# Seven of a head's complement masks by adding DMAs, their tiles taken later; output stores by sync

## Chip, cores and metric

One core of one Trainium2 chip. The metric is the device time of an execution in microseconds (us); the time before is the median of three runs.

## The reference, cut to what matters

Two graph layers over 2048 nodes with 512 features, each after a layer norm and a relu, each added to x. The first layer (related pairs, softmax over 1500 nodes, aggregation) is not touched. The second is an attention of 16 heads with a dense adjacency mask:

```
seq = (x @ W_seq).reshape(N, H, DH)              # N 2048, H 16, DH 32
scores = leaky_relu(score1[:, :, None] + score2[:, None, :], 0.2)
scores = scores + (1.0 - adj)[None, :, :] * MASK_VAL
attn = softmax(scores, axis=-1)
hidden = einsum('hij,jhd->ihd', attn, seq).reshape(N, D_IN) @ W_out + b_out
x = x + elu(hidden)
```

With leaky relu the exponential of a score is one of two products of a factor of i and a factor of j, by the sign of the sum. So a head needs, for each tile j of 128 columns, a mask of the neighbours whose sum is positive, and the rest of the neighbours: its complement within the adjacency.

## The kernel before

**Stages.** Stages 1 and 2 (to about 634 us) do the first layer, the projection to seq and the scores; `Heads` makes the factors, stores the score rows to DRAM and loads them back spread over the partitions. `stage4` (L1370 to 1616) is the 16 heads, `Output` (L1619 on) the last projection, elu and the stores.

**A head of stage 4.** Each head has 16 tiles j. `masks[:, j]` is one byte (fp8) per i, 2048 columns. ScalarE makes the sign mask of 13 tiles (L1443), VectorE that of tiles 3, 8 and 13 (`vector_sign`, L1484); VectorE ands each with the transposed adjacency `adjT` (`mask`, L1493), in the order 0 to 15. TensorE takes tile j in one of two ways. A **far** tile (the ten of `FAR`) has its own complement mask in `fars`: for each block of 128 rows it runs two matmuls of 99 columns, L1595 with the mask and L1596 with the complement. A **near** tile has none: L1598 multiplies the mask with 198 columns and L1599 the constant negated adjacency `nadjT` with 99. Complements come from `complement` (L1394): VectorE makes eight by xor (`far`, called one tile late), GpSimd two (tiles 3 and 5, `POOL_FAR`) by subtraction.

**Order.** TensorE walks j = 0 to 15 in two halves of the rows; the second half runs `LAG` = 4 tiles behind the first, so a head is 32 half-steps. A half fills four banks of psum; VectorE reduces them (`sum_parts`, L1506) in the middle of the next head, after its masks 3 and 5, and gives them free (`bank_free`), which the next head's first matmul of that half waits for. A mask slot may be written again when the second half has used it (`mask_used`; for the last tile `psum_done[1]`). VectorE also makes the values of the next head (`values`, two `take_off`), packed by ScalarE (`pack`, L1432), and scales, joins and norms the head before.

**Queues.** SP loads the row of scores of head n + 2 when head n's masks are all made (1 MB after spreading), and the x tiles for the output. GpSimd makes its complements and later issues the sixteen output stores (L1727). In stage 2 SP's last stores of x come before `heads.sync`, which stores the score rows (L1276) and loads the first two (L1280).

Of the kernel before, what the change touches and what calls it, by code (L numbers as in the profile page):

```python
# [20 lines left out]
U8 = mybir.dt.uint8  # L21
F8 = mybir.dt.float8e4
# [449 lines left out]
def stage2(nc, c, io, t, s, ps, f, heads, begin):  # L472
# [55 lines left out]
    with nc.Block() as block:  # L528
        @block.sync
        def _(sp):  # L530
# [77 lines left out]
            heads.sync(sp)  # L608
# [476 lines left out]
        def _(dve):  # L1085
# [135 lines left out]
            dve.wait_ge(masked, HA * ET)  # L1221
            for i, j in enumerate(NEAR_TILES):
# [142 lines left out]
NS = NT - len(VECTOR_SIGN)  # L1365
# [4 lines left out]
def stage4(nc, c, io, t, s, ps, output):  # L1370
# [18 lines left out]
    pool_far = sem("pool_far")  # L1389
    summed, scaled, joined, inverse = sem("summed"), sem("scaled"), sem("joined"), sem("inverse")  # L1390
    normed = t["normed"]

# [5 lines left out]
    with nc.Block() as block:  # L1398
        @block.sync
        def _(sp):  # L1400
# [5 lines left out]
            for n in range(HB - 2):  # L1406
                sp.wait_ge(mask_ready, NT * (n + 1))
                load(n + 2, n % 2)
# [5 lines left out]
            for b in (2, 3):  # L1414
                output.load(sp, b)

        @block.gpsimd
        def _(pool):
            for n in range(HB):
                for j in POOL_FAR:  # L1420
                    pool.wait_ge(mask_ready, NT * n + j + 1)
                    complement(pool, j, ALU.subtract).then_inc(pool_far, 1)
            output.gpsimd(pool)

        @block.scalar
        def _(act):
# [7 lines left out]
            def head(n, b):  # L1434
                act.wait_ge(s1_in[b], 8 * (n - b) + 16)
                for j in range(NT):
                    if j not in VECTOR_SIGN:

                        if j < NT - 1:
                            act.wait_ge(mask_used, (NT - 1) * n + j + 1)  # L1440
# [6 lines left out]
                    if j in (9, 14) and n < HB - 1:  # L1447
                        pack(n + 1, 1 - b, 0 if j == 9 else 1)
# [5 lines left out]
        def _(dve):  # L1454
# [26 lines left out]
            def vector_sign(n, b, j):  # L1481
                dve.wait_ge(mask_used, (NT - 1) * n + j + 1)
# [4 lines left out]
            def mask(n, j):  # L1487
                if j in VECTOR_SIGN:
                    dve.wait_ge(vector_signs, len(VECTOR_SIGN) * n + VECTOR_SIGN.index(j) + 1)
                else:  # L1490
                    dve.wait_ge(signs, NS * n + sum(x not in VECTOR_SIGN for x in range(j)) + 1)
# [42 lines left out]
            def head(n, b):  # L1534
                for j in range(NT):
                    if j + 1 in VECTOR_SIGN:
# [4 lines left out]
                    if n > 0:  # L1541
                        if j == 3:
                            sum_parts(n - 1, 0)
                        if j == 5:
# [8 lines left out]
                    if n < HB - 1:  # L1553
                        if j == 1:
                            values(n + 1)
                        if j == 9:
                            take_off(n + 1, 1 - b, 0)
                        if j == 11:
# [17 lines left out]
        def _(pe):  # L1576
            pe.sem_inc(mask_used, NT - 1)  # L1577

            def step(n, b, half, j):

                base = 4 * half
                if j == 0:
                    pe.wait_ge(bank_free[half], n + 1)
                pe.wait_ge(mask_ready, NT * n + j + 1)
                if j in POOL_FAR:
                    pe.wait_ge(pool_far, len(POOL_FAR) * n + POOL_FAR.index(j) + 1)
                elif j in FAR:
                    pe.wait_ge(far_ready, len(VECTOR_FAR) * n + VECTOR_FAR.index(j) + 1)
                for i in range(HT):
                    cols = slice(half * HALF + i * P, half * HALF + (i + 1) * P)  # L1590
                    out = ps[:, base + i // 2, 256 * (i % 2):256 * (i % 2) + 3 * CZ].rearrange("p (s c) -> p s c", s=3)
                    first = dict(start=(j == 0 and i % 2 == 0), stop=False, skip_group_check=True)
                    then = dict(start=False, stop=(j == NT - 1), skip_group_check=True)
# [6 lines left out]
                if j == NT - 1:  # L1600
                    last.then_inc(psum_done[half], 1)
                if half and j < NT - 1:
# [16 lines left out]
class Output:  # L1619
# [104 lines left out]
    def gpsimd(self, pool):  # L1724
        for it in range(NT):
            pool.wait_ge(self.done, it + 1)
            pool.dma_start(self.out[it * P:(it + 1) * P, :], self.x(it)).then_inc(self.y_out, 16)  # L1727
        pool.wait_ge(self.y_out, 16 * NT)


def build(nc, io, out, kind="Internal"):
# [4 lines left out]
        "adj_chunks": dram("adj_chunks", [NT, P, N], F8),  # L1736
    }
    with ExitStack() as c:
# [7 lines left out]
        t["adjT_in"], t["seq_in"] = (c.enter_context(nc.semaphore(n)) for n in ("adjT_in", "seq_in"))  # L1746
        t["rstd"] = c.enter_context(nc.sbuf_tensor("rstd", [P, 2, NT], F32))
# [50 lines left out]
```

## Time and profile before

| | us |
|---|---|
| median of three runs | 1166.32 (1164.46 to 1168.64) |
| the profiled execution | 1169.42 |
| its span | 1167.0 |
| busy: TensorE, VectorE, ScalarE, GpSimd | 1080.7, 949.3, 809.0, 163.1 |
| stage 4, about | 634 to 1096 |

The mean granted clock of TensorE is 0.979 of full speed. Busy time of TensorE is modelled from its matmuls' starts, and a few per cent of its records can be missing, so pace is read from starts. "By starts" below means from one instruction's start to the next one's on the same engine.

### The profile page before, as it was taken

How to read it: one execution, taken by the hardware profiler on the slowest of the kernel's cores; microseconds unless marked ns; L12 is line 12 of the kernel's file. 1: busy time of each engine (PE TensorE's matmuls, PEld its weight loads, DVE VectorE, ACT ScalarE, POOL GpSimd, SP SyncE). 2: the span in 40 equal slices, each digit the busy share in tenths (PEclk: the TensorE clock that was granted, in tenths of full speed). 3: DMA queues.
4: the chain of work that ended last, by engine and by line, in shares of the span. 5: the costliest groups of instructions: out<-in, count | busy, mean ns of one | idle time of the engine just before them, and what ended most of it. 6: DMA issues, size and time to landing. Idle time of an engine off the chain costs nothing. (4 is left out here: it accounts for less than half of the span.)

```text
span 1167.0 us, 24746 instructions
## 1 busy us (share of the span) xinstructions
PE 1080.7 (93%) x10565; PEld 738.8 (63%) x10565; DVE 949.3 (81%) x1323; ACT 809.0 (69%) x843; POOL 163.1 (14%) x174
## 2 busy tenths in 40 slices
PE   1999986999999999999996999999999999999997
PEld 1444432444444444444443999999999999999743
DVE  2355336899999999998834899999999999999565
ACT  1334326677777777775525999999999999999122
POOL 2788640000000000000000100100110000000011
PEclk9999996999999999999997899999999999999999
DMA  9630452322221121000433011110111111111311
GB/s 340 142 26 2 110 104 68 75 57 66 66 66 43 42 57 57 28 37 27 163 126 131 38 38 38 38 39 38 38 38 38 39 38 38 38 39 38 110 72 72
DMA packets 38269, 77.69 MB, mean 67 GB/s; under 512 B 5653, under 2 KB 15250, under 8 KB 36114
## 3 DMA queue, kind: packets, MB, share of 16 engines
q1 hardware_dynamic: 31954, 67.62, 16.1%
q0 software_dynamic: 6208, 8.50, 6.0%
q8 instruction: 84, 1.38, 0.5%
q14 instruction: 23, 0.19, 0.1%
HBM read 65.39 MB, written 23.21 MB: 76 GB/s over the span
## 5 line engine op out<-in xcount | busy, mean ns | idle before, releaser
L1443 ACT ACTIVATE area_h<-area_a,keep 128x2048 fp8e4<-128x2048 f32 x208 | 396.9, 1987 | 0.5 <-PEq L1577 0.5
L1595 PE MATMUL psum<-s_V,area_h 128*128 128x99 bf16 x2560 | 254.5, 210 | 21.1 <-issue 10.9
L1595 PEld LDWEIGHTS psum<-s_V,area_h 128*128 128x128 fp8e4 x2560 | 237.4, 98 | 25.2 <-issue 22.8
L1598 PE MATMUL psum<-s_V,area_h 128*128 128x198 bf16 x1536 | 218.7, 249 | 0.0
L1599 PE MATMUL psum<-s_V,late 128*128 128x99 bf16 x1536 | 212.8, 209 | 0.0
L1596 PE MATMUL psum<-s_V,area_b 128*128 128x99 bf16 x2048 | 205.5, 210 | 0.0
L1596 PEld LDWEIGHTS psum<-s_V,area_b 128*128 128x128 fp8e4 x2048 | 190.3, 98 | 0.0
L737 PE MATMUL psum<-area_h,f_region 128*128 128x512 f32 x384 | 184.9, 596 | 0.0
L1493 DVE TENSOR_TENSOR area_h<-area_h,area_a 128x512 uint32<-128x512 uint32 x256 | 173.5, 688 | 9.1 <-ACT area_h L1443 4.6
L1159 DVE SCALAR_TENSOR_TENSOR f_region<-area_b,s_r,f_region 128x1500 f32<-128x1500 f32 x96 | 170.8, 1780 | 2.2
L1170 DVE CUSTOM_DVE_ANT_0 area_b<-psum,late 128x1500 f32<-128x1500 f32 x96 | 161.1, 1715 | 10.8 <-PE psum L652 10.6
L956 ACT ACTIVATE area_b<-area_b,s_negm 128x1500 f32<-128x1500 f32 x96 | 147.8, 1541 | 25.4 <-DVE s_negm L1170 24.3
L652 PE MATMUL psum<-area_a 64*128 64x512 f32 (+1 forms) x576 | 143.5, 633 | 14.0 <-DVE s_negm L1170 13.9
L1598 PEld LDWEIGHTS psum<-s_V,area_h 128*128 128x128 fp8e4 x1536 | 150.4, 98 | 0.2
L1599 PEld LDWEIGHTS psum<-s_V,late 128*128 128x128 fp8e4 x1536 | 150.1, 98 | 0.0
L156 POOL DMA_INDIRECT rel_planes<-f_ones,f_flat x80 | 99.8, 1247 | 56.0 <-issue 20.4
L1394 POOL TENSOR_TENSOR area_b<-area_a,area_h 128x512 uint32<-128x512 uint32 x32 | 41.0, 1281 | 452.8 <-DVE area_h L1493 452.8
L652 PEld LDWEIGHTS psum<-area_a 64*128 64x128 f32 x576 | 55.0, 198 | 76.0 <-issue 52.2
L737 PEld LDWEIGHTS psum<-area_h,f_region 128*128 128x128 f32 x384 | 65.0, 191 | 43.0 <-issue 43.0
L902 ACT ACTIVATE f_region<-psum 128x256 f32<-128x256 f32 x96 | 36.6, 381 | 79.5 <-PE psum L707 63.9
L431 PE MATMUL psum<-f_region 128*128 128x512 f32 x192 | 83.7, 595 | 5.3 <-DVE f_region L304 4.1
L431 PEld LDWEIGHTS psum<-f_region 128*128 128x128 f32 x192 | 36.1, 190 | 49.8 <-issue 43.3
(175 smaller groups left out, 1343.5 us busy)
## 6 DMA issues: line engine op xcount, KB each, us to landing
area_a<-s_rows SPq DMA_DIRECT2D x16, 1024.0 KB, 4.6
rel_planes<-f_h SPq DMA_DIRECT2D x3, 2304.0 KB, 15.9
late<-rel_planes SPq DMA_DIRECT2D x36, 192.0 KB, 2.6
area_h<-in_x SPq DMA_DIRECT2D x4, 1024.0 KB, 12.9
keep<-in_adj POOLq DMA_DIRECT2D x16, 256.0 KB, 6.6
f_region<-in_x SPq DMA_DIRECT2D x16, 256.0 KB, 4.7
x<-f_region SPq DMA_DIRECT2D x16, 256.0 KB, 2.0
area_a<-adj_chunks SPq DMA_DIRECT2D x4, 1024.0 KB, 9.1
```

The lines of the kernel that those rows point to most:

```text
L431: last = pe.matmul(ps[:, 4 + g % 4, :], wT[w][:, k, dt * P:(dt + 1) * P], hT[:, k, ch * 512:(ch + 1) * 512], start=(k == 0), stop=(k == KT ...
L652: return pe.matmul(ps[:, 3 * half + ch, 0:cols.stop - cols.start], qk[rows, Q, p, r * P:(r + 1) * P], qk[rows, K, p, cols], start=True, st ...
L737: last = pe.matmul(ps[:, 7 if r < ET - 1 else 0, :], WT[m % 2][:, b, :], h[:, 2 * m + b, :], start=(m == order[0] and b == 0), stop=(m == ...
L956: act.activation(ex[:, hd, 0:NREL], ex[:, hd, 0:NREL], ACT.Exp, bias=negm[:, b, hd:hd + 1], scale=-1.0, accum_out=zs[:, b, hd:hd + 1]).the ...
L1159: dve.scalar_tensor_tensor(w, ex[:, hd, 0:NREL], r8[:, hd:hd + 1], w, ALU.mult, ALU.add).then_inc(added if hd < HA - 1 else w_ready, 1)
L1170: dve.tensor_tensor_reduce(ex[:, hd, 0:NREL], ps[:, 3 * (hd % 2):3 * (hd % 2) + 3, :].rearrange("p c j -> p (c j)")[:, 0:NREL], low[r % 2] ...
L1443: act.activation(masks[:, j, :], s1b[:, b, :], ACT.Relu, bias=t["s2"][:, n, 0, j:j + 1], scale=BIG, saturate=False).then_inc(signs, 1)
L1493: dve.tensor_tensor(own, own, adjT[:, :, j, :].bitcast(U32), ALU.bitwise_and).then_inc(mask_ready, 1)
L1595: pe.matmul(out[:, :, 0:DZ], masks[:, j, cols], V[:, b, j, :, 0:DZ], **first)
L1596: last = pe.matmul(out[:, :, DZ:CZ], fars[FAR.index(j)][:, cols], V[:, b, j, :, DZ:CZ], **then)
L1598: pe.matmul(out, masks[:, j, cols], V[:, b, j, :, :], **first)
L1599: last = pe.matmul(out[:, :, DZ:CZ], nadjT[:, NEAR_TILES.index(j), cols], V[:, b, j, :, DZ:CZ], **then)
```

## The change

Twelve tiles are far instead of ten. Seven of them (`DMA_FAR`) get their complement by DMA: SP copies the tile's adjacency from DRAM (`far_rows`) into the slot of `fars` when the slot has been used, and when the mask is ready GpSimd issues a DMA that adds the mask to that copy, as 16-bit integers. An entry of the adjacency is 0x40 (2.0), and so is one of the mask; 0x40 + 0x40 is 0x80, which is minus zero. VectorE makes three complements (6, 13, 14), GpSimd two (5, 7). TensorE walks the tiles in a new order, `TURN`, in which most tiles made by DMA come one to three places after their number. VectorE makes three signs in even heads and four in odd ones. VectorE's reductions of psum go from after masks 3 and 5 to after 5 and 7, the take_offs from 9 and 11 to 10 and 13, ScalarE's packs from 9 and 14 to 11 and 15. In stage 2 VectorE makes seven copies of adjacency tiles, and SP stores them to DRAM ahead of the score rows. The output stores are issued by SP instead of GpSimd.

```diff
+            for d, j in enumerate(DMA_FAR):
+                sp.wait_ge(t["apart"], d + 1)
+                sp.dma_start(t["far_rows"][d], t["fars"][FAR.index(j)]).then_inc(t["far_begun"][d], 16)
             heads.sync(sp)
...
+            for j in DMA_FAR:
+                dve.tensor_scalar(t["fars"][FAR.index(j)].bitcast(U32).rearrange("p (t i) -> p t i", t=NT),
+                                  t["adjT"][:, :, j, :].bitcast(U32), 0, None, ALU.bitwise_or).then_inc(t["apart"], 1)
...
-VECTOR_SIGN = (3, 8, 13)
-FAR = (0, 1, 3, 5, 6, 7, 9, 11, 13, 14)
-POOL_FAR = (3, 5)
-VECTOR_FAR = tuple(j for j in FAR if j not in POOL_FAR)
+SIGN_TILES = ((3, 8, 13), (2, 6, 10, 14))
+FAR = (5, 6, 7, 13, 14, 0, 1, 3, 8, 9, 11, 12)
+POOL_FAR = (5, 7)
+DMA_FAR = (0, 1, 3, 8, 9, 11, 12)
+VECTOR_FAR = tuple(j for j in FAR if j not in POOL_FAR + DMA_FAR)
+TURN = (2, 0, 4, 1, 5, 6, 3, 7, 10, 8, 9, 13, 14, 11, 15, 12)
...
+            def begin_far(n, d):
+
+                place = TURN.index(DMA_FAR[d])
+                if place < NT - 1:
+                    sp.wait_ge(mask_used, (NT - 1) * (n + 1) + place + 1)
+                else:
+                    sp.wait_ge(psum_done[1], n + 1)
+                sp.dma_start(fars[FAR.index(DMA_FAR[d])], t["far_rows"][d]).then_inc(far_begun[d], 16)
+            for n in range(HB - 1):
+                for j in TURN[:NT - LAG]:
+                    if j in DMA_FAR:
+                        begin_far(n, DMA_FAR.index(j))
+                if n < HB - 2:
+                    sp.wait_ge(mask_ready, NT * (n + 1))
+                    load(n + 2, n % 2)
+                for j in TURN[NT - LAG:]:
+                    if j in DMA_FAR:
+                        begin_far(n, DMA_FAR.index(j))
...
             for n in range(HB):
-                for j in POOL_FAR:
+                for j in sorted(POOL_FAR + DMA_FAR):
                     pool.wait_ge(mask_ready, NT * n + j + 1)
-                    complement(pool, j, ALU.subtract).then_inc(pool_far, 1)
-            output.gpsimd(pool)
+                    if j in POOL_FAR:
+                        complement(pool, j, ALU.subtract).then_inc(pool_far, 1)
+                    else:
+                        d = DMA_FAR.index(j)
+                        pool.wait_ge(far_begun[d], 16 * (n + 1))
+                        pool.dma_start(fars[FAR.index(j)].bitcast(U16), masks[:, j, :].bitcast(U16), accum_op=ALU.add).then_inc(far_added[d], 16)
...
                 if j in POOL_FAR:
                     pe.wait_ge(pool_far, len(POOL_FAR) * n + POOL_FAR.index(j) + 1)
+                elif j in DMA_FAR:
+                    pe.wait_ge(far_added[DMA_FAR.index(j)], 16 * (n + 1))
...
-    def gpsimd(self, pool):
+    def store(self, sp):
         for it in range(NT):
-            pool.wait_ge(self.done, it + 1)
-            pool.dma_start(self.out[it * P:(it + 1) * P, :], self.x(it)).then_inc(self.y_out, 16)
-        pool.wait_ge(self.y_out, 16 * NT)
+            sp.wait_ge(self.done, it + 1)
+            sp.dma_start(self.out[it * P:(it + 1) * P, :], self.x(it)).then_inc(self.y_out, 16)
+        sp.wait_ge(self.y_out, 16 * NT)
```

## Rows read from the trace of the kernel before

**Rows 1.** One head: busy us (instructions) of each engine, clock, DMA share, GB/s
```profile
785.80:814.00 28.20, 27.41 (x515) 27.25 (x514) 27.87 (x38) 26.77 (x16) 2.54 (x3) 1.00 0.10 40
```
**Rows 2.** Waits of VectorE and ScalarE, 660 to 1090 us: total, times, longest
```profile
DVE area_h L1493 <- ACT area_h L1443: 2.4, 3, 1.2
...
ACT s_V L1432 <- DVE s_tmp L1479: 12.8, 11, 1.2
```
**Rows 3.** Order of time at the borders of a head: start, us, engine, line, operation
```profile
785.57 1.80 DVE L1506 TENSOR_REDUCE s_sums<-psum 128x528 f32<-128x1584 f32 x1
...
786.63 0.21 PE L1599 MATMUL psum<-s_V,late 128*128 128x99 bf16 x1
787.63 0.21 PE L1595 MATMUL psum<-s_V,area_h 128*128 128x99 bf16 x1 [0.79 <-issue]
...
815.84 0.21 PE L1595 MATMUL psum<-s_V,area_h 128*128 128x99 bf16 x1 [0.77 <-issue]
```
**Rows 4.** Order of time on TensorE: far pairs, then near pairs
```profile
802.38 0.21 PE L1595 MATMUL psum<-s_V,area_h 128*128 128x99 bf16 x1
...
802.84 0.21 PE L1595 MATMUL psum<-s_V,area_h 128*128 128x99 bf16 x1
...
804.21 0.25 PE L1598 MATMUL psum<-s_V,area_h 128*128 128x198 bf16 x1
...
804.73 0.25 PE L1598 MATMUL psum<-s_V,area_h 128*128 128x198 bf16 x1
```
**Rows 5.** Order of time on VectorE: a sign, a mask, a complement
```profile
791.28 1.28 DVE L1484 TENSOR_SCALAR area_h<-area_a,keep 128x2048 fp8e4<-128x2048 f32 x1
792.47 0.69 DVE L1493 TENSOR_TENSOR area_h<-area_h,area_a 128x512 uint32<-128x512 uint32 x1
793.08 0.69 DVE L1394 TENSOR_TENSOR area_b<-area_a,area_h 128x512 uint32<-128x512 uint32 x1
```
**Rows 6.** Order of time on ScalarE: nine signs in a row
```profile
797.76 17.13 ACT L1443 ACTIVATE area_h<-area_a,keep 128x2048 fp8e4<-128x2048 f32 x9
```
**Rows 7.** DMA queue, 701.2 to 1067.9 us: packets, MB, share of 16 engines
```profile
q1 hardware_dynamic: 2256, 13.63, 10.0%
```
**Rows 8.** DMA queue of GpSimd, 300 to 500 us (four adjacency loads): packets, MB, share
```profile
q0 software_dynamic: 576, 1.05, 6.6%
```
**Rows 9.** DMA issues of the page: queue, count, KB each, median us to landing
```profile
keep<-in_adj POOLq DMA_DIRECT2D x16, 256.0 KB, 6.6
...
x<-f_region SPq DMA_DIRECT2D x16, 256.0 KB, 2.0
...
out<-area_h POOLq DMA_DIRECT2D x8, 256.0 KB, 2.3
```
**Rows 10.** Order of time: a DMA issue on GpSimd and VectorE beside it
```profile
309.45 0.53 POOL L145 DMA_DIRECT2D keep<-in_adj  x1 [32.90 <-ACT f_region L943]
...
309.66 3.60 DVE L1159 SCALAR_TENSOR_TENSOR f_region<-area_b,s_r,f_region 128x1500 f32<-128x1500 f32 x2
```
**Rows 11.** That VectorE operation in the page's groups: busy us, mean ns, idle before
```profile
L1159 DVE SCALAR_TENSOR_TENSOR f_region<-area_b,s_r,f_region 128x1500 f32<-128x1500 f32 x96 | 170.8, 1780 | 2.2
```
**Rows 12.** Order of time in head 0: GpSimd's complement and VectorE's mask beside it
```profile
645.38 1.65 POOL L1394 TENSOR_TENSOR area_b<-area_a,area_h 128x512 uint32<-128x512 uint32 x1 [68.17 <-DVE area_h L1493]
...
646.39 1.18 DVE L1493 TENSOR_TENSOR area_h<-area_h,area_a 128x512 uint32<-128x512 uint32 x1 [0.50 <-ACT area_h L1443]
```
**Rows 13.** Order of time on VectorE and SP at the end of stage 2
```profile
591.31 2.10 DVE L1223 TENSOR_SCALAR late<-area_a 128x512 uint32<-128x512 uint32 x6
...
591.42 2.54 SPq L606 DMA_DIRECT2D area_b<-seq_rows  x4
...
598.70 0.69 DVE L1114 TENSOR_TENSOR f_region<-f_region,psum 128x512 f32<-128x512 f32 x1 [5.29 <-PE psum L737]
...
599.41 19.89 SPq L541 DMA_DIRECT2D x<-f_region  x2
...
626.97 0.80 SPq L1276 DMA_DIRECT2D s_rows<-f_region  x2
```

More of the change, by code:

```diff
@@ L21 @@
 U8 = mybir.dt.uint8
+U16 = mybir.dt.uint16
 F8 = mybir.dt.float8e4
@@ L1221, in _ @@
             dve.wait_ge(masked, HA * ET)
+            dve.wait_ge(w_ready, ET)
             for i, j in enumerate(NEAR_TILES):
@@ L1389, in stage4, with vector_signs_made @@
     pool_far = sem("pool_far")
+    far_begun = t["far_begun"]
+    far_added = [sem(f"far_added{d}") for d in range(len(DMA_FAR))]
     summed, scaled, joined, inverse = sem("summed"), sem("scaled"), sem("joined"), sem("inverse")
     normed = t["normed"]
+    def vector_signs_made(n):
+        return sum(len(SIGN_TILES[m % 2]) for m in range(n))
     def complement(engine, j, take):
@@ L1405, in _ @@
                          ).then_inc(t["wout_in"], 16)
-            for n in range(HB - 2):
-                sp.wait_ge(mask_ready, NT * (n + 1))
-                load(n + 2, n % 2)
+            def begin_far(n, d):
[15 more added lines that the diff above has]
+                        begin_far(n, DMA_FAR.index(j))
             for b in range(2):
@@ L1415, in _ @@
                 output.load(sp, b)
+            output.store(sp)
         @block.gpsimd
@@ L1436, in head @@
                 for j in range(NT):
-                    if j not in VECTOR_SIGN:
-                        if j < NT - 1:
-                            act.wait_ge(mask_used, (NT - 1) * n + j + 1)
+                    if j not in SIGN_TILES[n % 2]:
+                        if TURN.index(j) < NT - 1:
+                            act.wait_ge(mask_used, (NT - 1) * n + TURN.index(j) + 1)
                         elif n > 0:
@@ L1446, in head @@
                         pack(0, 0, j)
-                    if j in (9, 14) and n < HB - 1:
-                        pack(n + 1, 1 - b, 0 if j == 9 else 1)
+                    if j in (11, 15) and n < HB - 1:
+                        pack(n + 1, 1 - b, 0 if j == 11 else 1)
             for n in range(HB):
@@ L1487, in mask @@
             def mask(n, j):
-                if j in VECTOR_SIGN:
-                    dve.wait_ge(vector_signs, len(VECTOR_SIGN) * n + VECTOR_SIGN.index(j) + 1)
+                if j in SIGN_TILES[n % 2]:
+                    dve.wait_ge(vector_signs, vector_signs_made(n) + SIGN_TILES[n % 2].index(j) + 1)
                 else:
-                    dve.wait_ge(signs, NS * n + sum(x not in VECTOR_SIGN for x in range(j)) + 1)
+                    dve.wait_ge(signs, NT * n - vector_signs_made(n) + sum(x not in SIGN_TILES[n % 2] for x in range(j)) + 1)
                 own = masks[:, j, :].bitcast(U32).rearrange("p (t i) -> p t i", t=NT)
@@ L1541, in head @@
                     if n > 0:
-                        if j == 3:
+                        if j == 5:
                             sum_parts(n - 1, 0)
-                        if j == 5:
+                        if j == 7:
                             sum_parts(n - 1, 1)
@@ L1577, in _, with step @@
             pe.sem_inc(mask_used, NT - 1)
-            def step(n, b, half, j):
-                base = 4 * half
-                if j == 0:
+            def step(n, b, half, place):
+                base, j = 4 * half, TURN[place]
+                if place == 0:
                     pe.wait_ge(bank_free[half], n + 1)
@@ L1591, in step @@
                     out = ps[:, base + i // 2, 256 * (i % 2):256 * (i % 2) + 3 * CZ].rearrange("p (s c) -> p s c", s=3)
-                    first = dict(start=(j == 0 and i % 2 == 0), stop=False, skip_group_check=True)
-                    then = dict(start=False, stop=(j == NT - 1), skip_group_check=True)
+                    first = dict(start=(place == 0 and i % 2 == 0), stop=False, skip_group_check=True)
+                    then = dict(start=False, stop=(place == NT - 1), skip_group_check=True)
                     if j in FAR:
@@ L1599, in step @@
                         last = pe.matmul(out[:, :, DZ:CZ], nadjT[:, NEAR_TILES.index(j), cols], V[:, b, j, :, DZ:CZ], **then)
-                if j == NT - 1:
+                if place == NT - 1:
                     last.then_inc(psum_done[half], 1)
-                if half and j < NT - 1:
+                if half and place < NT - 1:
                     last.then_inc(mask_used, 1)
@@ L1746, in build @@
         t["adjT_in"], t["seq_in"] = (c.enter_context(nc.semaphore(n)) for n in ("adjT_in", "seq_in"))
+        t["apart"] = c.enter_context(nc.semaphore("apart"))
+        t["far_begun"] = [c.enter_context(nc.semaphore(f"far_begun{d}")) for d in range(len(DMA_FAR))]
         t["rstd"] = c.enter_context(nc.sbuf_tensor("rstd", [P, 2, NT], F32))
```

11 lines of the change are left out of this document (5 added, 6 removed).

## The prediction

> **What bounds the kernel now.** I read the heads of stage 4 first, because all of the change but its preparation and its last stores lies there, and because head follows head in one pattern from 673 to 1068 us. In the table of stretches [rows 1] one head of 28.20 us has TensorE busy for 27.41, VectorE for 27.87, ScalarE for 26.77. Three engines within 6% of one another: the shares don't say which one sets the pace, so the second view is who waits. Over fourteen heads VectorE waits 2.4 us in all; ScalarE waits about a microsecond a head, for VectorE [rows 2]. VectorE's 27.87 and the rest of the period are its own semaphore hops between dependent steps. The third view is the border between two heads [rows 3]. TensorE starts its last matmul of a head at 786.63 and the first of the next at 787.63, where 0.05 would do: a hole of 0.95. The chain calls it "issue", but it ends right behind VectorE's reduction of psum, 785.57 to 787.37, which gives the banks free. TensorE finished these banks about five of its 32 half-steps before the end of the head (a step is one tile of one half); VectorE comes to them late, after mask 3. So **VectorE sets the period of 28.21 us** (787.63 to 815.84) and TensorE alone would take 28.21 - 0.95 = 27.26.
>
> **The change, part by part.** Everything is per head, times 15 periods.
>
> TensorE: far tiles go from 10 to 12 of 16. A far pair (99 + 99 columns) takes 0.092 us, five of them from 802.38 to 802.84; a near pair (198 + 99) takes 0.130, four from 804.21 to 804.73 [rows 4]. Two tiles are 32 pairs: 32 x 0.038 = 1.2 us less. TensorE alone: 26.05.
>
> VectorE: its complements go from 8 to 3 (tiles 6, 13, 14), its signs from 3 to 3 and 4 in turn. By starts, a mask costs 0.61 and a sign 1.19; a complement has the mask's 0.69 of busy time and so its 0.6 [rows 5]. So 28.21 - 5 x 0.60 + 0.5 x 1.19 = 25.8 on average, 25.2 in a head with three signs and 26.4 in one with four. It is now ahead of TensorE, and waits for it at the two reductions, moved from j = 3 and 5 to 5 and 7. A head with four signs is 0.35 over TensorE's 26.05, the next gives back 0.85. Counted from the end of the head before, VectorE has far 13 done after about 12.7 us in the dear head (a reduction, 1.95 with its hops; masks 8 to 14; two signs; two take_offs and scale, about 1.2 each; a complement) and TensorE asks for it at place 11, half-step 18 of 32, 14.7 us: 2 us to spare cover that.
>
> ScalarE: 12.5 signs for 13, each 1.90 (nine in 17.13), beside two packs [rows 6]: 26.77 - 0.95 = 25.8. Its wait for VectorE shrinks as VectorE is earlier. Sign 12 now waits for the very end of the head (place 15); it has more than 20 us before it is used, and what queues behind it is 14, 15 and the next head's, all early too.
>
> So three engines at 26.05, 25.8 and 25.8. I take a **period of 26.1**: 15 x (28.21 - 26.1) = 31.7 us. The 1.2 of the columns alone would have given 18; the rest is the hole and the room on VectorE, since both must fall for the period to fall.
>
> What has to carry this is the DMA work, and no row of before shows an adding DMA. Seven plain copies from DRAM of 256 KB and seven additions per head. Engine time of plain traffic: 13.63 MB took 10.0% of 366.7 us on all sixteen engines [rows 7], 2.7 us a MB, 0.7 us a copy. An addition moves three times 256 KB (two reads and a write), so it costs at least 0.7. The nearest row that does arithmetic on the way is the load of the adjacency with its conversion from float32: four in 200 us took 6.6% [rows 8], 3.3 us each, for 262,144 elements and 1 MB read. That is the upper bound. An addition handles 131,072 two-byte elements and reads half a MB, so I take half, 1.65. Sum: 7 x 1.65 + 7 x 0.7 + 2.7 for the score row = 19 us of 26.1: they fit. The Trainium skill (Collectives: The Full Stack, on why ReduceScatter is half of AllGather) says that the add itself is free and that its second source read halves the rate; by that an addition is 1.4, an estimate from the page, and the sum stays.
>
> Latency: a 256 KB store from the gpsimd queue lands after 2.3 us, the converting load after 6.6 [rows 9]. The addition must land between mask and matmul. Tile 8 is the tightest: its mask is ready 2.6 us after the border (reduction 1.95, mask 0.60), it is taken at place 9, half-step 14 of 32, 11.4 us: 8.8 us. Tile 9 has 9.9, the others over 10. I take 4 to 5 us; even 6.6 and 0.6 of issue fit. The copy before it starts as soon as the slot is free, at half-step 24 of the head before, 9 us ahead of the mask.
>
> GpSimd: issuing takes it 0.53 us [rows 10], seven times, beside two complements that take 2.54 together [rows 1]: 6.3 of 26 us. Queued behind its waits are only its own later tiles, in the order in which masks come. Does it slow VectorE? The load issued at 309.45 lies over a VectorE operation with SBUF inputs at 309.66 which took 1.80 by starts, as the mean of all its kind, 1.78 [rows 10, 11]: no. A complement on GpSimd does: beside the one at 645.38 a mask took 1.18 for 0.69 [rows 5, 12]. Tile 5's comes before the reduction, which reads psum, as now; tile 7's is behind VectorE's far 6, then the reduction. I cost it at nothing; uncovered it is 0.5 us a head. The Trainium skill (SBUF — State Buffer, Who interferes with whom) speaks against the change: while VectorE runs in a two-port mode, gpsimd can't write its descriptors. By it an issue might be held for one sign. No row here shows that for a sign, and the sum would stay, within tile 8's 8.8 us.
>
> **Once only.** VectorE makes seven copies and four near tiles where it now makes six near tiles: 5 more of 0.35 (six in 2.10), before 598.70, where it sat idle 5.29 [rows 13]: hidden. SP issues seven stores behind its last x store (619.3), some 0.6 each as the four loads from 591.42 on, until 623.7, and the stores drain 1.8 MB in about 5 us (at the 2.7 a MB above), to about 626; the score rows go out at 626.97 [rows 13]. Free, at worst 3 us, since the first sign waits for those rows. Head 0: TensorE begins with tile 2, later than now with tile 0, but without the hole that follows, and it has 1.2 us less to do: I take 1.0, between -1 and 2. Last store: issued by sync, its landing is 2.0, as that of an x store, instead of 2.3 [rows 9]: 0.3. Sum: 31.7 + 1.0 + 0.3 = 33.0. The profiled execution took 1169.4 with its span of 1167.0 and lies 3.1 above the median 1166.3: it would become 1136.4, the median 1133.3.
>
> **The rivals.** (1) **The additions are slow, and the DMA engines become the bound; slower than before.** If one takes 3.3, as the conversion does, the sum is 23.1 + 7.4 = 30.5 a head: 15 x 2.3 = 35 us more, near 1200. It decides at (28.21 - 7.4) / 7 = 3.0 us an addition against before, and from 2.7 on it takes from the gain. For it: the only row of such work is 3.3. Against: that load reads a whole MB. TensorE would wait at far tiles 8, 9 for DMA. (2) **The additions fit but land late** for tile 8 or 9, by bunching with the score row (2.7 us of all engines) and the copies for 11 and 12, or VectorE pays half a microsecond here and there: a period of 26.5 to 27.6, 1142 to 1158. (3) **VectorE was no bound**, the hole is TensorE's own: then only the columns count, 27.0 a head, 1148. Against it is that the reduction ends where the hole ends. I count it within (2). (4) The additions come nearly free and head 0 gains more: 1129. That is in my forecast's own range, 1129 to 1140.
>
> **How the numbers follow.** Forecast 0.57; rivals (2) and (3), 0.20, faster but for a small tail; a case near no change, a period of 28, 0.04; rival (1), 0.19. A measurement of this kernel can't tell 0.3%, 3.5 us, from no change. Faster 0.76, same 0.04, slower 0.20. The range reaches from 1128 over the forecast and (2) to 1160 and leaves out (1).
>
> **What would show it.** Right: a period of 26.0 to 26.3 with no hole at the border, VectorE with short waits for TensorE before its reductions, the clock at 1.00, about 0.7 share of DMA. Wrong: TensorE waiting for a DMA at tiles 8 or 9, or GpSimd's issue far above 0.6 us; a DMA share above 0.95; VectorE's masks above 0.69 us beside the issues. The one step whose failure turns the sign is the 1.65 us of an addition.

## The result

The kernel after takes **1131.67 us** (median of four runs, 1129.99 to 1135.75), the kernel before 1166.78 beside it: a ratio of 0.9705, interval 0.9672 to 0.9738. The forecast was 1133.3, with a range of 1128 to 1160.

Part of a difference between two traces isn't the change's. The first sign of stage 4 starts at 634.84 us in the trace of before and at 627.87 in that of after. The last x store but one starts 5.5 us apart already (599.41 and 593.88), and from it to the score rows both need 27.5 us, as do all twelve variants below. The cause lies in stage 1, where the code is the same: up to 140 us VectorE's operations start within 0.5 us of one another in the two traces, from 207 us on they are 7.2 apart. Between the traces of this study the first sign varies from 627.9 to 634.8. So I cut each trace at its first sign. From there on:

| kernel | first sign to first reduction of psum | to the projection (15 heads) | to VectorE's end | to the end | sum |
|---|---|---|---|---|---|
| before | 37.9 | 423.3 | 66.7 | 4.3 | 532.2 |
| after | 38.7 | 392.5 | 66.7 | 2.4 | 500.3 |

That is 31.9 us, of which 30.8 lie in the heads, -0.8 in head 0 and 1.9 in the last store. The medians differ by 35.1. The 3 us more are most likely the first part's; the runs behind the medians have no traces that could show it.

**The profile after.** Two heads of after, in the table of stretches: length, busy us (instructions) of TensorE, its weight loads, VectorE, ScalarE, GpSimd, then clock, DMA share and GB/s. They answer to [rows 1].

```profile
795.28:821.67 26.39, 26.39 (x525) 26.39 (x523) 26.06 (x34) 26.39 (x16) 10.06 (x10) 1.00 0.76 183
821.67:847.18 25.51, 25.51 (x506) 25.51 (x503) 25.05 (x34) 25.51 (x15) 9.94 (x10) 1.00 0.73 188
```

TensorE is busy all of the time, at a granted clock of 1.00, the 2.4 GHz level. The two heads take 51.9 us, 25.95 each; over fifteen, from TensorE's first matmul of head 1 (668.70) to the projection (1059.14), it is 26.03. ScalarE is as full here, but it has room: the variant with three signs puts its own work at 25.6. The hole of [rows 3] is gone. In the waits, 660 to 1060 us (total, times, longest), the engines but GpSimd, whose waits for masks are left out, show this:

```profile
...
ACT s_hT L1747 <- PE psum L1721: 18.8, 1, 18.8
DVE s_sums L1541 <- PE psum L1633: 10.4, 6, 8.8
ACT area_h L1478 <- PE psum L1633: 2.7, 4, 0.7
PEld psum L1635 <- issue: 1.9, 1, 1.9
PE psum L1635 <- DVEq L1545: 1.8, 1, 1.8
```

ScalarE's 18.8 and VectorE's longest, 8.8, belong to the end of the last head. Within the heads the direction has turned against [rows 2]: VectorE and ScalarE wait for TensorE, if at all (VectorE once for ScalarE, 0.6 us), and TensorE waits once, for the reduction that gives the banks of head 0 free. It never waits for a DMA. The DMA work, 701.2 to 1037 us (packets, MB, share of 16 engines; then issues with count, KB each, median us to landing), answers to [rows 7] and [rows 9]:

```profile
q0 software_dynamic: 13104, 23.86, 41.4%
q1 hardware_dynamic: 15083, 36.96, 32.7%
...
late<-area_h POOLq DMA_DIRECT2D x52, 256.0 KB, 4.4
late<-far_rows SPq DMA_DIRECT2D x52, 256.0 KB, 4.5
area_a<-s_rows SPq DMA_DIRECT2D x12, 1024.0 KB, 7.2
area_b<-far_rows SPq DMA_DIRECT2D x39, 256.0 KB, 3.5
area_b<-area_h POOLq DMA_DIRECT2D x39, 256.0 KB, 4.8
```

The gpsimd queue carries nothing there but 91 additions: 0.414 x 335.8 / 91 = **1.53 us of all sixteen engines each**. The sync queue takes 109.8 us, of which 13 MB-sized loads at 2.8 (36.7 us for 13 in [rows 7]) are 36.7; the 91 copies are 0.80 each. The additions land after 4.4 and 4.8 us.

### The profile page after: what moved, and what is told of

Its sections match the earlier page's. It is cut to its first block, busy times and chain, and to the rows that moved or that the text cites. A ratio compares the mean times of both kernels' runs of the same rounds, so it can differ in the third digit from the quotient of the medians.

```text
span 1128.2 us, 25108 instructions
## 1 busy us (share of the span) xinstructions
PE 1051.7 (93%) x10560; PEld 716.5 (64%) x10565; DVE 914.3 (81%) x1256; ACT 791.8 (70%) x835; POOL 271.7 (24%) x272
## 3 DMA queue, kind: packets, MB, share of 16 engines
q1 hardware_dynamic: 50386, 101.19, 25.6%
## 4 chain that ended last, share of the span: by engine, by line
PE 58%; DVE 9%; issue 9%; ACT 8%; DMA 1%; DVEq 0%; SPq 0%
PE psum L1632 12%; PE psum L1633 12%; PE psum L741 7%; PE psum L1635 7%; PE psum L656 7%; PE psum L1730 5%; PE psum L1636 4%; DVE area_b L1174 3%; DVE f_region L1163 3%; ACT area_h L1478 3%; ACT area_b L960 2%; ACT f_region L947 2%; PE psum L711 1%; PE psum L761 1%; PE psum L1721 1%
## 5 line engine op out<-in xcount | busy, mean ns | idle before, releaser
L1478 ACT ACTIVATE area_h<-area_a,keep 128x2048 fp8e4<-128x2048 f32 x200 | 382.3, 1988 | 4.8 <-PE psum L1633 2.7
L1632 PE MATMUL psum<-s_V,area_h 128*128 128x99 bf16 x3072 | 298.3, 209 | 1.4 <-DVE area_b L1408 1.4
L1632 PEld LDWEIGHTS psum<-s_V,area_h 128*128 128x128 fp8e4 x3072 | 283.4, 98 | 1.9 <-DVE area_h L1528 1.3
L1528 DVE TENSOR_TENSOR area_h<-area_h,area_a 128x512 uint32<-128x512 uint32 x256 | 168.5, 687 | 12.1 <-ACT area_h L1478 7.5
L1635 PE MATMUL psum<-s_V,area_h 128*128 128x198 bf16 x1024 | 150.6, 249 | 13.8 <-DVE area_h L1528 12.1
L656 PE MATMUL psum<-area_a 64*128 64x512 f32 (+1 forms) x576 | 138.5, 615 | 10.3 <-DVE s_negm L1174 10.2
L1636 PE MATMUL psum<-s_V,late 128*128 128x99 bf16 x1024 | 145.4, 209 | 0.0
L1635 PEld LDWEIGHTS psum<-s_V,area_h 128*128 128x128 fp8e4 x1024 | 100.4, 98 | 14.9 <-issue 14.7
L1633 PE MATMUL psum<-s_V,late 128*128 128x99 bf16 x1024 | 105.0, 209 | 0.0
L1636 PEld LDWEIGHTS psum<-s_V,late 128*128 128x128 fp8e4 x1024 | 100.2, 98 | 0.0
L1458 POOL DMA_DIRECT2D area_b<-area_h x48 | 49.1, 1058 | 199.7 <-DVE area_h L1528 199.7
L1633 PEld LDWEIGHTS psum<-s_V,late 128*128 128x128 fp8e4 x1024 | 94.4, 97 | 0.0
```

Of the source, the lines that this page charges most:

```text
L656: return pe.matmul(ps[:, 3 * half + ch, 0:cols.stop - cols.start], qk[rows, Q, p, r * P:(r + 1) * P], qk[rows, K, p, cols], start=True, st ...
L1478: act.activation(masks[:, j, :], s1b[:, b, :], ACT.Relu, bias=t["s2"][:, n, 0, j:j + 1], scale=BIG, saturate=False).then_inc(signs, 1)
L1528: dve.tensor_tensor(own, own, adjT[:, :, j, :].bitcast(U32), ALU.bitwise_and).then_inc(mask_ready, 1)
L1632: pe.matmul(out[:, :, 0:DZ], masks[:, j, cols], V[:, b, j, :, 0:DZ], **first)
L1633: last = pe.matmul(out[:, :, DZ:CZ], fars[FAR.index(j)][:, cols], V[:, b, j, :, DZ:CZ], **then)
L1635: pe.matmul(out, masks[:, j, cols], V[:, b, j, :, :], **first)
```

## The experiments

Every variant ran beside the kernel before; its ratio is to that. "Period" is the spacing of TensorE's last matmul of one head and of the next: that of the steady heads, or, where they vary, the mean from head 1 to head 15. (A fifteenth of the way from the first reduction to the projection would mislead: that reduction comes 3.7 us behind TensorE's half with nine by DMA, 0.2 with nine by DMA and signs.) "Segment" is first sign to end, 532.2 for before and 500.3 for after; each segment is that of one trace.

| variant | median us | ratio, interval | period of a head | segment |
|---|---|---|---|---|
| columns alone | 1181.4 | 1.0119 (1.0093 to 1.0144) | 29.41 | 548.0 |
| relief alone | 1154.1 | 0.9887 (0.9861 to 0.9912) | 27.24 | 518.5 |
| stores by gpsimd | 1136.8 | 0.9735 (0.9703 to 0.9768) | 26.0 | 502.8 |
| plain order | 1136.4 | 0.9741 (0.9707 to 0.9775) | 26.0 | 501.6 |
| three signs | 1141.2 | 0.9809 (0.9768 to 0.9850) | 26.56 | 508.3 |
| six idle additions | 1147.9 | 0.9857 (0.9816 to 0.9897) | 27.0 | 513.9 |
| ten by DMA | 1130.6 | 0.9710 (0.9675 to 0.9745) | 25.8 | 494.5 |
| nine by DMA | 1128.8 | 0.9693 (0.9655 to 0.9731) | 25.55 | 494.0 |
| six signs in head 0 | 1133.5 | 0.9699 (0.9663 to 0.9735) | 26.0 | 497.8 |
| nine by DMA and signs | 1125.0 | 0.9639 (0.9599 to 0.9678) | 25.5 | 491.1 |
| reductions early | 1158.1 | 0.9926 (0.9903 to 0.9949) | 27.8 | 523.8 |
| before, reductions late | 1172.1 | 1.0039 (1.0024 to 1.0055) | 28.54 | 538.7 |

### Which engine set the pace

**Columns alone**: the kernel before with the twelve far tiles and nothing else.

```diff
-FAR = (0, 1, 3, 5, 6, 7, 9, 11, 13, 14)
+FAR = (0, 1, 3, 5, 6, 7, 8, 9, 11, 12, 13, 14)
```

> The kernel before with twelve far tiles (8 and 12 added), their two complements made by VectorE; no DMA, no new order. TensorE has 1.2 us less to do in a head, VectorE 1.2 us more. Theory A (VectorE set the period of 28.2 us): the period becomes 28.2 + 2 x 0.60 = 29.4, 18 us more in 15 heads, 1184. Theory B (the hole between heads is TensorE's own and only columns count): 27.0 a head, 1148. No change in time would mean that the two are bound together in another way.

Measured: 1181.4, slower by 1.2%. The stretch 700 to 1035 us and the waits in it (columns as above):

```profile
700.00:1035.00 335.00, 303.45 (x5836) 297.55 (x5837) 331.10 (x444) 304.57 (x173) 29.70 (x24) 1.00 0.10 37
```
```profile
ACT s_V L1432 <- DVE s_tmp L1479: 30.4, 12, 2.8
PE psum L1595 <- ACT s_V L1432: 20.0, 11, 1.8
PE psum L1595 <- DVE late L1394: 10.4, 33, 0.5
```

TensorE has less to do than before and waits; VectorE is as busy as before (331.07 us of the same stretch). The period is 29.41 us = 28.21 + 2 x 0.60: two complements of VectorE more, to the hundredth. Fewer columns, paid for with complements of VectorE, lose time while VectorE sets the pace, which was the reading of [rows 3].

**Relief alone**: the kernel after with ten far tiles, five of them by DMA, so VectorE and ScalarE are relieved and the columns are those of before.

```diff
-FAR = (5, 6, 7, 13, 14, 0, 1, 3, 8, 9, 11, 12)
+FAR = (5, 6, 7, 13, 14, 0, 1, 3, 8, 11)
-DMA_FAR = (0, 1, 3, 8, 9, 11, 12)
+DMA_FAR = (0, 1, 3, 8, 11)
```

> The changed kernel with ten far tiles as before (9 and 12 are near again), so five additions by DMA; VectorE, ScalarE and the order as in the changed kernel. TensorE has as many columns as before. Theory A: VectorE is relieved, the hole goes, TensorE's own 27.25 us set the period: 15 x (28.2 - 27.25) less than before and 15 x 1.2 more than the changed kernel, 1150. Theory B (only columns count): 1166, as before.

Measured: period 27.24; the prediction's TensorE alone was 27.26. TensorE is busy for 335.00 of 335 us and VectorE waits for it, 18 times, 15.3 us. So the gain of the change has two parts, about 14 us of relief (the reductions' new place and the last store with it) and 18 of columns, and the second exists only behind the first.

**Before, reductions late**: the kernel before with only the reductions moved, from after masks 3 and 5 to after 5 and 7.

> The kernel before with only the reductions moved, from after masks 3 and 5 to after 5 and 7, as in the change. The run with the reductions early in the kernel after took a period of 27.95 for 26.0, so their place matters there; here it is asked what it does alone. Theory A (VectorE sets the period of before by its own work and never waits for TensorE, so it can't gain by coming later; TensorE only gets its banks later once): period 28.2 within 0.3, 1164 to 1171. Theory B (GpSimd's complement of tile 5 now lies under the reduction, which reads psum, and no longer over a mask): up to 0.5 to 1.1 us less of VectorE a head, period 27.1 to 27.7, 1150 to 1160. Rival C (the banks come free 1.8 us later in each head and TensorE can't make it up): period 29 or more, 1180 and above.

Measured: period 28.54, slower by 0.4%. TensorE gets its banks later in every head and still keeps to VectorE's pace, so it had been no bound. The 0.33 us more are on VectorE: its mask behind the reduction takes 1.02 us for 0.68, because GpSimd's complements of tiles 3 and 5 now run back to back past the end of the reduction. In order of time (start, us):

```profile
843.07 3.46 POOL L1394 TENSOR_TENSOR area_b<-area_a,area_h 128x512 uint32<-128x512 uint32 x2 [25.08 <-DVE area_h L1493]
...
844.11 1.80 DVE L1506 TENSOR_REDUCE s_sums<-psum 128x528 f32<-128x1584 f32 x1
...
846.05 1.02 DVE L1493 TENSOR_TENSOR area_h<-area_h,area_a 128x512 uint32<-128x512 uint32 x1
```

Theory A holds but for this term; B had its sign wrong, since the complement was well placed in the kernel before.

**Reductions early**: the kernel after with the reductions back at 3 and 5.

```diff
-                        if j == 5:
+                        if j == 3:
                             sum_parts(n - 1, 0)
-                        if j == 7:
+                        if j == 5:
                             sum_parts(n - 1, 1)
```

> The kernel after with VectorE's two reductions of psum back after masks 3 and 5, where they stood before. Theory A (the room on VectorE and the columns make the gain, the place of the reductions doesn't): VectorE waits once for TensorE and from then on works 1.2 us later against it, which only takes from the lead of the masks; period 26.0 to 26.2, 1132 to 1135. Rival B (the move of the reductions is what took the hole away): VectorE waits about 2 us for TensorE at each first reduction, can't make it up, and the hole or waits for tiles 4 to 9 come: period 26.8 or more, 1143 and above.

Measured: periods of 28.0 and 27.55 in turn, 27.8 on average, 1158.1 us. **My theory A fell**, and by the most of this study: without the new place of the reductions the kernel after is 26 us slower by the medians, 23.5 by the segments, of a gain of 35 and 31.9. The view of the waits, 700 to 1035 us, names a loop:

```profile
PE psum L1632 <- DVE area_b L1408: 14.3, 24, 1.8
...
DVE s_sums L1541 <- PE psum L1633: 9.5, 19, 0.7
```

TensorE waits for a complement of VectorE, and VectorE for TensorE, in the same head. In order of time:

```profile
854.89 0.21 PE L1632 MATMUL psum<-s_V,area_h 128*128 128x99 bf16 x1 [1.24 <-DVE area_b L1408]
...
862.67 1.81 DVE L1541 TENSOR_REDUCE s_sums<-psum 128x528 f32<-128x1584 f32 x1 [0.35 <-PE psum L1633]
...
866.66 1.81 DVE L1541 TENSOR_REDUCE s_sums<-psum 128x528 f32<-128x1584 f32 x1 [0.74 <-PE psum L1633]
...
881.62 0.68 DVE L1408 TENSOR_TENSOR area_b<-area_a,area_h 128x512 uint32<-128x512 uint32 x1
...
890.23 1.81 DVE L1541 TENSOR_REDUCE s_sums<-psum 128x528 f32<-128x1584 f32 x1 [0.36 <-PE psum L1633]
```

From the first reduction to far 13 (881.62 + 0.68) VectorE needs 19.6 us; from far 13 TensorE needs 7.9 to the end of the half whose reduction comes next. Round the loop that is 27.5, which is the period of this head; in a head with four signs it is half a microsecond more. In the kernel after the same way, 795.28 to 811.10 + 0.68, is 16.5: the loop would take 24.4 and doesn't bind. The 3.1 between the two ways are two masks that now stand behind the reduction (1.2), the second reduction's wait (0.74), and 1.1 of a mask beside GpSimd's complement of tile 7, which the next head shows by itself:

```profile
897.91 1.65 POOL L1408 TENSOR_TENSOR area_b<-area_a,area_h 128x512 uint32<-128x512 uint32 x1 [1.89 <-DVE area_h L1528]
...
898.35 1.76 DVE L1528 TENSOR_TENSOR area_h<-area_h,area_a 128x512 uint32<-128x512 uint32 x1
```

In the kernel after that complement, 799.79 for 1.65 us, lies under the reduction at 800.23, which takes its usual 1.80. A mask reads SBUF twice and is held, from 0.69 to 1.76; a reduction that reads psum isn't. The Trainium skill (SBUF — State Buffer, Who interferes with whom) has this as a rule: a VectorE instruction with two SBUF inputs contends with a GpSimd one that reads SBUF, a reduction never does. These rows agree.

### What the additions cost

**Six idle additions**: the kernel after with six more additions a head, behind its own, into buffers that stage 4 doesn't use (of the edit, the clearing of these buffers and GpSimd's wait for the additions of the head before are left out here).

```diff
+                        if d < 6 and n < HB - 2:
+                            pool.dma_start(idle_sum[d].bitcast(U16), nadjT[:, 0, :].bitcast(U16), accum_op=ALU.add).then_inc(idle_added, 16)
```

> The kernel after with six more additions of 256 KB in each of heads 0 to 13, issued by GpSimd right behind its own, into buffers that stage 4 doesn't use: they are no part of the computation. It asks where rival (1) of the prediction begins. Theory A (an addition costs 1.53 us of all sixteen engines however many there are, and engine time adds up): 13 x 1.53 + 8.5 us of copies and score row = 28.4 us a head, more than the period of 26.0, so the DMA engines become the bound: period 28.4 or more, 15 heads x 2.4 = 35 us, some 1167, with TensorE waiting for late additions. GpSimd has 13 x 0.9 + 3 = 15 us of issue and stays under. Rival B (the 1.53 is mostly waiting, and additions side by side overlap): share of DMA under 1, period within 0.5 us of 26.0, under 1140.

Measured: 1147.9 us, a period of 27.0. The same stretch and the queues in it:

```profile
700.00:1035.00 335.00, 324.95 (x6326) 322.30 (x6324) 322.61 (x402) 321.09 (x183) 183.64 (x182) 1.00 1.01 234
```
```profile
q0 software_dynamic: 22921, 41.74, 70.9%
q1 hardware_dynamic: 14327, 35.85, 29.5%
...
late<-area_h POOLq DMA_DIRECT2D x52, 256.0 KB, 8.1
```

The DMA engines are full (a share of 1.01), an addition lands after 8.1 us for 4.4, and TensorE idles. 237.5 us for 157 additions are 1.51 each, as before, so engine time does add up. The sum was too high, 28.4 for 27.0: a copy is 0.75 here where I took 0.83 (by 98.8 us, 12 loads and 86 copies), which makes 27.7, and the shares of busy engines add to a little more than 1. Theory A in kind; in time 14 us of segment for the 35. This is the mechanism of rival (1), and it takes six additions more to bring it about. One caution: GpSimd waited 85.8 us for extra additions to land, so part of the lateness is the order in which this variant issues.

**Ten by DMA** and **nine by DMA**: thirteen far tiles (10 as well), with ten or nine complements by DMA, one or two by VectorE; with ten, VectorE also makes four signs in every head.

```diff
-FAR = (5, 6, 7, 13, 14, 0, 1, 3, 8, 9, 11, 12)
+FAR = (5, 6, 7, 13, 14, 0, 1, 3, 8, 9, 10, 11, 12)
-DMA_FAR = (0, 1, 3, 8, 9, 11, 12)
+DMA_FAR = (0, 1, 3, 8, 9, 10, 11, 12, 14)
-TURN = (2, 0, 4, 1, 5, 6, 3, 7, 10, 8, 9, 13, 14, 11, 15, 12)
+TURN = (2, 0, 4, 1, 5, 6, 3, 7, 8, 9, 10, 13, 11, 15, 14, 12)
```

> The kernel after with a thirteenth far tile (10) and ten complements by DMA instead of seven; VectorE makes one complement (13) and four signs in every head, GpSimd two. Theory A (DMA engine time adds up): 10 x 1.53 + 10 x 0.83 + 2.7 for the score row = 26.3 us a head, over the 25.4 that TensorE would need with one far tile more (32 half pairs, 0.6 us less than 26.0): period 26.3 to 27, later than the kernel after by 0 to 15 us, 1132 to 1150, and TensorE waits for additions. Rival B (DMA isn't near its bound): period 25.4, 15 x 0.6 = 9 us faster than the kernel after, 1123.

> The kernel after with a thirteenth far tile (10) and nine complements by DMA instead of seven; VectorE makes two (6, 13) and three and four signs in turn, GpSimd two. DMA: 9 x 1.53 + 9 x 0.83 + 2.7 = 23.9 us a head; TensorE 25.4, ScalarE 25.8, VectorE about 25.2. Theory A (the sum of the terms holds): ScalarE sets a period of 25.8, 15 x 0.2 = 3 us faster than the kernel after, 1129, if no addition comes late; a share of DMA of 0.93 makes lateness likely, then 1132 to 1145. Rival B (TensorE's columns alone count): period 25.4, 1123.

The diff is that of nine. Measured, the stretch of each, ten first:

```profile
700.00:1035.00 335.00, 332.88 (x6695) 331.82 (x6694) 326.86 (x405) 326.68 (x185) 169.36 (x158) 1.00 1.03 248
```
```profile
700.00:1035.00 335.00, 333.96 (x6708) 332.94 (x6706) 325.76 (x410) 335.00 (x191) 154.38 (x144) 1.00 0.95 229
```

With ten the DMA engines are full, at a share of 1.03, and TensorE waits for an addition eight times in stage 4, 4.7 us in all: 25.8 a head where seven of its fourteen take the 25.4 that it needs. Expectation A held in kind and not in size: its period was 26.3 to 27 and its time at best that of the kernel after, whose segment is 5.8 us longer. With nine the engines are at 0.95 and ScalarE is the bound, busy for 335.00 of 335 with TensorE close behind it: 25.55, forecast 25.8. Nine saves 6.3 us of the segment against after.

### The other terms

**Three signs**: VectorE makes signs 3, 8, 13 in every head, ScalarE thirteen.

```diff
-SIGN_TILES = ((3, 8, 13), (2, 6, 10, 14))
+SIGN_TILES = ((3, 8, 13), (3, 8, 13))
```

> The kernel after, but VectorE makes three signs in every head (tiles 3, 8, 13), not three and four in turn; ScalarE makes 13 in every head. Theory A (three engines stand close together, and ScalarE has no more room than the terms of the sum give it): ScalarE needs 13 signs of 1.90 and two packs, 26.8 us a head, and becomes the bound: period 26.8 for 26.0, first sign to end 500 + 8 to 11 = about 510, some 1142 us. Rival B (ScalarE's room is larger than I summed, and VectorE's fourth sign buys nothing): period 26.0, within 2 us of the kernel after, 1132.

Measured: period 26.56, segment + 8.0. ScalarE becomes the bound, as A said; VectorE waits for it 31 times, 20.0 us in 390. Half a sign more, 0.95 us a head, costs 0.55 of period: 0.4 us was the whole room there was, and ScalarE's own work in the kernel after is 26.56 - 0.95 = 25.6 a head where the forecast had 25.8.

**Plain order**: the kernel after with `TURN` from 0 to 15.

> The changed kernel with TensorE taking tiles in the order 0 to 15. Theory A (a landing of 4.5 us is covered by the lead that VectorE has at the border, which is at mask 7 when TensorE begins a head): tile 8's mask is ready 2.6 to 3.8 us after the border, its sum 5.5 us later at 8.1 to 9.3, TensorE asks at half-step 12, 9.8 us: no loss, within 3 us of the changed kernel. Rival C (the order is what makes the DMA way work): a wait of 0.5 to 1.5 us a head at tile 8 or 9, 1140 to 1154.

Measured: the same period, segment + 1.3. Taking the tiles late isn't what makes it work; an addition that lands 4.5 us after its issue fits in the natural order too, but for one wait of 1.3 us.

**Stores by gpsimd**: the kernel after with the output stores back on GpSimd.

> The changed kernel with its output stores issued by gpsimd again. The forecast put the swap at 0.3 us (landing 2.3 against 2.0). The trace of the changed kernel has 2.4 us from VectorE's last operation to the end of the span, that of before 4.35: by that the swap is worth 1.9 us, and this run should show 4.3 again and a time 1.5 to 2 us longer, 1133.5. If the tail stays at 2.4, the difference came from something else.

Measured: VectorE's end to the end of the span 4.9 us for 2.4. The last issues of after, then of this variant (start, us):

```profile
1124.51 1.66 SPq L1764 DMA_DIRECT2D out<-area_h  x2
1125.12 0.69 DVE L1703 SCALAR_TENSOR_TENSOR area_h<-s_v,s_e 128x512 f32<-128x512 f32 x1
```
```profile
1130.32 0.69 DVE L1703 SCALAR_TENSOR_TENSOR area_h<-s_v,s_e 128x512 f32<-128x512 f32 x1
1131.31 0.54 POOL L1764 DMA_DIRECT2D out<-area_h  x1 [0.79 <-DVE area_h L1703]
```

The store from GpSimd is issued 0.3 us after VectorE's end and lands after 2.3, by 1133.6, yet the span ends at 1135.9. The view of line 1412, the end of the block, shows what comes between (duration in ns, start in us), first in the kernel after, then here:

```profile
L1412 SPq DRAIN  x1: 7/7/7, 1128.0 to 1128.0; - x1
```
```profile
L1412 POOLq DRAIN  x1: 1851/1851/1851, 1133.8 to 1133.8; - x1
```

An engine that has waited for its last store runs a DRAIN before the end: 0.01 us on SP, 1.85 on GpSimd (1.36 in the kernel before). The 2.4 us are 1.84 of this, 0.27 of a later issue and 0.27 of landing. What GpSimd's DRAIN waits for isn't shown.

**Six signs in head 0**: in head 0 VectorE makes six signs for three; the other heads have four and three in turn (where the list is read, `[n % 2]` becomes `[n]`, not shown).

```diff
-SIGN_TILES = ((3, 8, 13), (2, 6, 10, 14))
+SIGN_TILES = ((2, 4, 6, 8, 10, 12),) + ((2, 6, 10, 14), (3, 8, 13)) * 7 + ((2, 6, 10, 14),)
```

> The kernel after, but in head 0 VectorE makes six signs (tiles 2, 4, 6, 8, 10, 12) where it made three, ScalarE ten; the heads after it have four and three in turn. It tests what held head 0: I had reckoned that it gains 1.0 us and it lost 0.8. Theory A (ScalarE paces head 0: 13 signs and four packs, 28.5 us before it can begin head 1): mask 2 is ready about 2 us sooner, ScalarE begins head 1 some 5 us sooner, and first sign to first reduction falls from 38.7 to 33 to 36; the hole of 1.75 at the first border goes; first sign to end 500.3 - 4 to 6, some 1127 us. Rival B (TensorE paces it, by its low clock at the start and its own 26 us): first sign to first reduction stays within 1 us of 38.7.

Measured: 35.4 to the first reduction for 38.7, and no hole at the first border; the segment gains 2.5, not 4 to 6. ScalarE did pace head 0: from 630 to 666 us in the kernel after it is busy for 36.00 of 36, VectorE for 28.29 and TensorE for 27.95. Relieved of three signs it shares the pace with VectorE, which is now busy for 4.00 of 4 us, as ScalarE still is, in each stretch from 637 to 669. TensorE adds its own: it starts head 0 after ten microseconds of idleness at a granted clock of 0.50, the 1.2 GHz level, and comes to 1.00, 2.4 GHz, only after some microseconds of work:

```profile
637.00:641.00 4.00, 0.00 (x0) 0.00 (x0) 4.00 (x5) 4.00 (x3) 1.63 (x2) 0.50 0.69 217
641.00:645.00 4.00, 2.94 (x28) 2.85 (x29) 4.00 (x7) 4.00 (x3) 1.22 (x2) 0.50 0.48 87
645.00:649.00 4.00, 3.52 (x60) 3.37 (x59) 4.00 (x5) 4.00 (x4) 2.28 (x2) 0.91 0.38 70
```

**Nine by DMA and signs**: nine by DMA, six signs in head 0, then four, three, four in turn.

> The kernel with nine additions and thirteen far tiles, with six signs of VectorE in head 0 and then four, three, four in turn instead of three, four: all that the runs point to in one kernel. ScalarE 12.33 signs a head: 25.4 us; TensorE 25.4; VectorE 25.4; DMA 24.5 measured with nine. Theory A (the terms of the sum still hold this near to each other): period 25.75 - 0.3 = 25.5, fifteen heads 382 for 386, head 0 some 4 less: first sign to end 494 - 8 = 486, some 1121 us. Rival B (with all four within 1 us of one another small waits eat it): period 25.75 or more, and only head 0 gains, 1125.

Measured: 1125.0 us, the fastest kernel of the study, 0.9639 (0.9599 to 0.9678) of before where after is 0.9705; its segment is 9.2 us shorter than that of after. Against nine by DMA the segment is 2.9 us shorter. The long way over the first border, 28.2 us there, is 25.4 here and gives 2.8. The later heads give 1.0 in all, 25.47 on average for 25.55. And 1.0 is lost in head 0, where TensorE waits 2.34 us, up to 652.80, for an addition to land.

In ten of fourteen heads the period is TensorE's own 25.37, and from 700 to 1035 us it is busy for 334.65 us of 335, ScalarE for 333.25: TensorE's columns are the bound again, with all of the others close. GpSimd waits eleven times, 24.0 us, for a copy, and TensorE three times, 3.1 us, for an addition. Theory A's period of 25.5 came, but nine by DMA had all but reached it: the 25.75 that it was reckoned from holds the hole at the first border. In time this is rival B, 1125.

## Why the prediction was right

**The bound.** Right: VectorE set 28.21, TensorE alone 27.26 (27.24 measured with ten far tiles), and 26.05 with twelve (26.03). The same terms gave 29.41, 26.8 (26.56) and 25.8 (25.55) for variants; the two set by ScalarE are 0.25 too high. The forecast for fifteen heads was 31.7; measured is 30.8. With head 0 and the end the sum was 33.0; measured is 31.9, two misses against each other (below). The medians' 35.1 lies 2.1 over that sum and the traces' 31.9 lies 1.1 under it; by either the time is within about 2 us of the forecast.

**The addition.** 1.65 us was taken between 0.7 and 3.3; it is 1.53, and the landing 4.4 to 4.8 where I said 4 to 5. Half of the converting load was a guess from bytes and elements, and a lucky one as much as a good one. That it stands 1.9 times over a plain copy (1.53 to 0.80) is what the Trainium skill (Collectives: The Full Stack, on why ReduceScatter is half of AllGather) gives for two source reads and a free add; no run here tells the second read from the add. Copies are 0.80 and not 0.7. The DMA share is 0.75 for the 0.7 of the sum. The turning point against before was put at 3.0 us an addition, some 28 us of DMA work a head. The variant with six more additions was filled up at 27.0 us a head, where its time was still below that of before. (Rival (2)'s times are some 2 us high for its periods: 26.5 to 27.6 give 1139 to 1156 on the forecast's own terms.)

**GpSimd's issue: mis-sized.** 0.53 was taken from a load; an addition takes 0.85 where nothing is beside it. The step "does it slow VectorE: no" is right, but the reverse happens: beside a sign of VectorE an issue takes twice as long, 1.63 us. The Trainium skill (SBUF — State Buffer, Who interferes with whom) has this for a two-port mode of VectorE; whether a sign runs in one, no run here shows. In order of time in the kernel after:

```profile
794.45 0.85 POOL L1458 DMA_DIRECT2D area_b<-area_h  x1 [2.54 <-DVE area_h L1528]
```
```profile
716.25 1.63 POOL L1458 DMA_DIRECT2D area_b<-area_h  x1 [1.60 <-DVE area_h L1528]
...
716.49 1.27 DVE L1519 TENSOR_SCALAR area_h<-area_a,keep 128x2048 fp8e4<-128x2048 f32 x1
```

It cost nothing: GpSimd is busy for 10 us of 26 and the tiles had their 8.8 us.

**GpSimd's complements.** "I cost it at nothing" was right, and thinner than it sounded. They lie under the reductions, and the variant with the reductions early shows the uncovered price, 1.1 us for a mask and not 0.5. The prediction treated the move of the reductions as a detail; it is a condition. It did sum the way from the border to far 13 (12.7 of 14.7 us), but only for the new place, and not on to the end of the half and the next reduction, which is what decides whether two engines with room each still make a slow loop. In the new place this loop has 26.0 - 24.4 = 1.6 us left, in the old one none.

**Head 0: wrong sign.** 1.0 gain was forecast, 0.8 loss came. The step looked at TensorE's order and columns; head 0 is paced by ScalarE's 13 signs and four packs, so neither helps. On TensorE the first half of head 0 is done 34.9 us after the first sign for 34.7 before, all but the same; the 0.8 is the first reduction, which now stands two masks later, and a hole of 1.75 on TensorE comes behind it.

**The end: mis-sized.** 0.3 was forecast, from the landings in [rows 9]; it is 1.9 against before and 2.5 in the direct comparison. The landing isn't all that a last store costs: most of the rest is GpSimd's DRAIN.

**The start.** Right: in all kernels, with or without the seven copies and stores, the way from the x store to the score rows is 27.5 us.

## What to carry to other kernels

Before crediting fewer instructions on one engine, find which engine's end closes the gap between two rounds: here 18 us of TensorE's columns were worth nothing until VectorE had been relieved. Then walk the loop through both engines (reduction, last mask made, half done, next reduction) and not the busy sums alone: moving two reductions by two masks was worth 23.5 us of the segment, and in the kernel before, where VectorE set the pace alone, the same move cost 6.5 of it. DMA engines that lie idle can do a bitwise complement by addition, as long as their summed engine time stays under the period and the result has somewhat more than its landing time. In plain order tile 8 had 6.0 to 7.2 us, by the estimate in that expectation, for a landing of some 4.5, and TensorE waited once.

## What the runs showed of the hardware that I had not expected

- A GpSimd elementwise operation over a VectorE mask stretches the mask from 0.69 to 1.76 us, but a reduction from psum beside it keeps its 1.80. Work for GpSimd is best put where VectorE reads psum.
- A kernel whose last stores are issued by SP ends 2.4 us behind VectorE's last operation, with GpSimd 4.3 to 4.9. The landings alone, 2.0 and 2.3, don't tell this; GpSimd's DRAIN of 1.36 to 1.85 us does.
- Busy shares of the DMA engines in full use read 1.01 to 1.03. When they are full, a 256 KB addition lands after up to 6.5 us with ten by DMA and 8.1 with six idle ones, where it took 4.4 and 4.8 before.
- The same first part of a program started its second part up to 7 us apart (627.9 to 634.8) from one execution to another. In segments of the trace a difference of 1.3 us could be found, and the wait that made it; medians could not show it.
